# Attention products: which engine takes which heads, a bf16 copy of the softmax weights, and weight conversion in half-size rounds

## The reference

```
xn = layernorm(x)
q, k, v = xn @ wq.T, xn @ wk.T, xn @ wv.T        # each row: 16 heads x 128
q, k = rope(q), rope(k)
scores[s,h,t] = q[s,h,:] . k[s,t,:] / sqrt(128)  # 16 x 16 per row, between the heads of ONE row
attn[s,h,:]   = sum_t softmax_t(scores)[s,h,t] * v[s,t,:]
x = x + attn @ wo.T
y = layernorm(x)
g, u = y @ ((gate_w - 128) * gate_scale).T, y @ ((up_w - 128) * up_scale).T   # int32 weights, 8192 wide
x = x + (silu(g) * u) @ ((down_w - 128) * down_scale).T
```

## Time and profile before

| | us |
|---|---|
| median of 3 runs | 8804.4 |
| lowest and highest run | 8561.8 and 8891.8 |
| the profiled execution | 8532.4 |
| its span on the slowest core (the 8 cores: 8478.5 to 8530.8) | 8530.8 |
| phase A, up to about | 250 |
| phase B, three times, up to about | 1640 |
| phase CD, up to phase E's first matmul | 5072.2 |
| phase E | 3458.6 |

### The profile page before, as it was taken

One profiled execution on the slowest core, in us unless ns is written; L12 is line 12 of the kernel. 1 busy time (PEld: TensorE's weight loads), 2 busy tenths in 40 slices (PEclk: granted clock), 3 DMA queues, 4 the chain that ended last, 5 costly groups with the idle time before them and its releaser, 6 DMA issues.

```text
span 8530.8 us, 45886 instructions; the slowest of 8 cores (8478.5 to 8530.8 us)
## 1 busy us (share of the span) xinstructions
PE 4010.2 (47%) x17408; PEld 1773.4 (21%) x17408; DVE 1869.9 (22%) x1216; ACT 1162.6 (14%) x1257; POOL 1710.7 (20%) x443
## 2 busy tenths in 40 slices
PE   1264636400110111111110139966996699669966
PEld 0121212200000000000000014422442244224422
DVE  2000000044444444444445630000000000000000
ACT  3221212201111111111111011100110011001100
POOL 0000000054444444444446620000000000000000
PEclk9986868755555555555555569977997799779987
DMA  5444454411111111111111026645664566456644
GB/s 179 119 158 128 155 140 145 158 29 62 61 63 65 63 65 61 65 65 68 68 67 69 21 63 152 140 89 134 153 144 89 129 152 147 89 125 154 155 85 108
DMA packets 1714552, 892.33 MB, mean 105 GB/s; under 512 B 1626192, under 2 KB 1634416, under 8 KB 1679520
## 3 DMA queue, kind: packets, MB, share of 16 engines
q1 hardware_dynamic: 1639616, 713.09, 32.8%
q10 hardware_dynamic: 62976, 125.84, 3.8%
q0 software_dynamic: 11744, 50.46, 2.9%
HBM read 755.10 MB, written 167.77 MB: 108 GB/s over the span
## 4 chain that ended last, share of the span: by engine, by line
PE 41%; DMA 20%; POOL 13%; DVE 11%; issue 9%; ACT 5%; ACTq 1%; SPq 0%; DVEq 0%; POOLq 0%
POOL prod L88 13%; PE ps_dn L97 12%; PE ps_g L97 10%; PE ps_u L97 10%; PE ps_p L97 5%; DMA wdb<-wd_sc 5%; DVE prod L88 4%; DVE sc_sb L88 2%; DVE red L88 2%; DMA cvin<-uwT 2%; PE ps_y L97 2%; ACT cvout L88 2%; DMA cvin<-gwT 2%; DMA kt<-k_sc 2%; DMA wg_sc<-cvout 1%
## 5 line engine op out<-in xcount | busy, mean ns | idle before, releaser
L97 PE MATMUL ps_y<-wo_bf,aTs 128*128 128x512 bf16 x1024 | 293.2, 457 | 2587.5 <-ACT yrow_t L88 2281.2
L97 PE MATMUL ps_dn<-h_sb,wdb 128*128 128x512 bf16 x4096 | 1059.1, 427 | 479.9 <-DMA wdb<-wd_sc 474.1
L97 PE MATMUL ps_p<-wst,xnT 128*128 128x512 bf16 x3072 | 769.4, 417 | 622.5 <-ACT prow L88 328.7
L88 DVE TENSOR_REDUCE sc_sb<-prod 128x16 f32<-128x2048 bf16 x256 | 584.2, 2285 | 2073.8 <-POOL prod L88 2065.6
L88 POOL TENSOR_TENSOR prod<-p_sb,vt 128x2048 bf16<-128x2048 f32 x176 | 943.8, 5415 | 356.3 <-DVE p_sb L88 356.3
L97 PE MATMUL ps_g<-xn2q,wgb 128*128 128x512 bf16 x4096 | 934.0, 381 | 66.0 <-DMA wgb<-wg_sc 66.0
L88 POOL TENSOR_TENSOR prod<-qt,kt 128x2048 bf16<-128x2048 bf16 x176 | 720.4, 4132 | 1191.3 <-DMA kt<-k_sc 1154.6
L97 PE MATMUL ps_u<-xn2q,wub 128*128 128x512 bf16 x4096 | 925.8, 379 | 0.8 <-DMA wub<-wu_sc 0.8
L116 POOL DMA_DIRECT2D out_rows<-outt x16 | 8.6, 536 | 3548.9 <-DVE outt L88 3452.6
L88 DVE TENSOR_REDUCE red<-prod 128x128 f32<-128x2048 bf16 x256 | 585.2, 2286 | 591.2 <-POOL prod L88 583.0
L97 PEld LDWEIGHTS ps_y<-wo_bf,aTs 128*128 128x128 bf16 x1024 | 114.2, 114 | 2762.6 <-issue 2687.5
(11 more groups left out here) (52 smaller groups left out, 937.2 us busy)
## 6 DMA issues: line engine op xcount, KB each, us to landing
wgb<-wg_sc SPq DMA_DIRECT2D x256, 512.0 KB, 5.2
wub<-wu_sc SPq DMA_DIRECT2D x256, 512.0 KB, 5.1
wdb<-wd_sc SPq DMA_DIRECT2D x128, 1024.0 KB, 7.0
cvin<-gwT SPq DMA_DIRECT2D x64, 1024.0 KB, 8.0
cvin<-uwT SPq DMA_DIRECT2D x64, 1024.0 KB, 8.3
cvin<-dwT SPq DMA_DIRECT2D x64, 1024.0 KB, 7.6
wg_sc<-cvout ACTq DMA_DIRECT2D x64, 512.0 KB, 2.6
wu_sc<-cvout ACTq DMA_DIRECT2D x64, 512.0 KB, 2.6
```

Of the source, the lines that this page charges most:

```text
L88: ins = getattr(self.h, opname)(*args, **kw)
L97: ins = self.h.matmul(*args, **kw)
```

## The change

Three things are changed, together.

1. **Which engine takes which heads.** VectorE multiplies heads 0 to 4 and GpSimd heads 5 to 15, in both halves of `stage1`. The counts (5 and 11) stay.
2. **A bf16 copy of the weights.** The normalization writes a new tile `pbf` in bf16 in place of overwriting `p_sb`, and the attention products read `pbf`. Its waits for the previous tile's products move from the exponential to the normalization.
3. **Conversion rounds.** A round is 128 x 1024 instead of 128 x 2048: 384 rounds of a 512 KB load and a 256 KB store, with four buffers; a load waits for the conversion four rounds back. There are still two load streams (`b % 2`) and one store stream, so a load also waits for the landing of the load two rounds back. The calls per place go from 2 to 4 (phase A), from 2 to 3 (phase B), and from 3 to 6 (both places of phase CD). That is 32 + 144 + 192 = 368 rounds; the last 16 are left to the drain.

```diff
+        cvin = [cv_sb.enter_context(nc.sbuf_tensor(f"cvin{i}", [128, 1024], I32))
+                for i in range(4)]
...
-                b = r % 2
-                ld = em.dma("sync", f"d_fc{b}", cvin[b][:],
+                b = r % 4
+                ld = em.dma("sync", f"d_fc{b % 2}", cvin[b][:],
...
                 cv = em.do("scalar", "activation", cvout[b][:], cvin[b][:],
                            AF.Copy, bias=-128.0,
-                           waits=[(f"d_fc{b}", ld), ("d_fcs", M["cv_st"][b])])
+                           waits=[(f"d_fc{b % 2}", ld),
+                                  ("d_fcs", M["cv_st"][b])])
...
         def phaseA():
             for g in range(8):
-                conv_step(2)
+                conv_step(4)
...
             for st in range(NT):
-                conv_step(2)
+                conv_step(3)
...
-                    peng = "gpsimd" if hh < POOL_SC else "vector"
+                    peng = "vector" if hh < H - POOL_SC else "gpsimd"
...
                 ex = em.do("scalar", "activation", p_sb[:], sc_sb[:], AF.Exp,
                            scale=INV_SQRT_HD,
-                           waits=[("vector", last_sc), ("vector", M["p_used"]),
-                                  ("gpsimd", M["p_used_g"])])
+                           waits=[("vector", last_sc),
+                                  ("vector", M["p_used"])])
...
-                pn = em.do("vector", "scalar_tensor_tensor", p3, p3, 1.0,
+                pb3 = pbf.ap().rearrange("p (hh t) -> p hh t", hh=H)
+                pn = em.do("vector", "scalar_tensor_tensor", pb3, p3, 1.0,
                            bc_ap(rden_sb, 0, [[1, 16], [0, 16]]),
-                           ALU.mult, ALU.mult, waits=[("vector", rd)])
+                           ALU.mult, ALU.mult,
+                           waits=[("vector", rd), ("gpsimd", M["p_used_g"]),
+                                  ("vector", M["pbf_used_v"])])
...
-                    peng = "gpsimd" if hh < POOL_AT else "vector"
-                    pbc = bc_ap(p_sb, hh * 16, [[0, 128], [1, 16]])
+                    peng = "vector" if hh < H - POOL_AT else "gpsimd"
+                    pbc = bc_ap(pbf, hh * 16, [[0, 128], [1, 16]])
...
-                conv_step(3)
+                conv_step(6)
...
-                conv_step(3)
+                conv_step(6)
```

More of the change, by code:

```diff
@@ L248, in build @@
         cv_sb = contextlib.ExitStack()
[L249 to L252, removed]
+        cvin = [cv_sb.enter_context(nc.sbuf_tensor(f"cvin{i}", [128, 1024], I32))
+                for i in range(4)]
+        cvout = [cv_sb.enter_context(nc.sbuf_tensor(f"cvout{i}", [128, 1024], BF16))
+                 for i in range(4)]
         CONV_ROUNDS = []
@@ L256, in build @@
             for _rh in range(_mat.shape[0] // 128):
-                for _cb in range(_mat.shape[1] // 2048):
+                for _cb in range(_mat.shape[1] // 1024):
                     CONV_ROUNDS.append((_mat, _cache, _rh, _cb))
@@ L267, in conv_step @@
                 mat_ap, cache, rh, cb = CONV_ROUNDS[r]
-                b = r % 2
-                ld = em.dma("sync", f"d_fc{b}", cvin[b][:],
+                b = r % 4
+                ld = em.dma("sync", f"d_fc{b % 2}", cvin[b][:],
                             mat_ap[rh * 128:(rh + 1) * 128,
-                                   cb * 2048:(cb + 1) * 2048],
+                                   cb * 1024:(cb + 1) * 1024],
                             waits=[("scalar", M["cv_m"][b])])
@@ L278, in conv_step @@
                             cache.ap()[rh:rh + 1, :,
-                                       cb * 2048:(cb + 1) * 2048].rearrange(
+                                       cb * 1024:(cb + 1) * 1024].rearrange(
                                 "o p c -> p (o c)"),
@@ L283, in conv_step @@
                 M["conv_done"] = st
-        M.update(cv_r=0, cv_m=[0, 0], cv_st=[0, 0], conv_done=0)
+        M.update(cv_r=0, cv_m=[0] * 4, cv_st=[0] * 4, conv_done=0)
         xnT_scope = contextlib.ExitStack()
@@ L405, in build @@
         p_sb = sbc("p_sb", [128, 256], F32)
+        pbf = sbc("pbf", [128, 256], BF16)
         den_sb = sbc("den_sb", [128, 16], F32)
@@ L427, in build @@
                  sc_done=0, att_done=[0, 0],
-                 exp_done=0, p_used=0, p_used_g=0,
+                 exp_done=0, p_used=0, p_used_g=0, pbf_used_v=0,
                  scp_done_p=[0, 0], scp_done_vv=[0, 0],
@@ L544, in stage1 @@
                 att_last = red_last
-                M["p_used"] = max(pn, atv)
+                M["p_used"] = pn
                 M["p_used_g"] = atg
+                M["pbf_used_v"] = atv
                 M["vt_used"][bi] = atg
```

## The result

| | before | after |
|---|---|---|
| median of all runs (32 of each, side by side) | 8872.9 | 8923.6 |
| lowest run | 8529.0 | 8564.4 |
| ratio of like executions, 95% interval | | 1.0043 [1.0022, 1.0063] |
| the profiled execution | 8532.4 | 8579.0 |
| its span on the slowest core | 8530.8 | 8577.4 |

The change costs 0.4%, about 37 us; a gain of 78 was forecast. In more than half of the executions of either kernel the cores of one die have a lower granted clock and take some per cent longer, which puts the medians above the interval given and above both profiled executions; the ratio compares like with like.

What follows compares the result with a forecast made beforehand. Phase CD bounds it as a chain passing between engines, none near full. Terms of -112.2 (tile 0 to 15), -24.9 (tile 0), +77.1 (tail) and -18 (phase B) sum to -78, from 8532.4 to 8454 us; range 8290 to 8740.

Steps and rivals of the forecast that it cites:

- rival 3: Order of heads, phase CD: if GpSimd wins each contest, the halves end at 59.3 and 86.1, total 8523; 1 in 10.
- bf16: Attention products in phase CD's second half: prices stay at 5.36 and 3.62 us, set by the read step; nothing taken.
- rival 1: Second half of phase CD: bf16 copy cuts products to the scores half's prices, 430 us less, 8024; 2 in 10.
- c: Conversion rounds: time from one store's issue to the next, taken as 2.5 us between bounds 2.06 and 3.43.
- 197 cycles: Store cycles on the path: 16 in phase A, 96 in B, 85 in CD and after it.
- 23 first stores: First store of each conversion group, taken at 4.0 us, half of 8.04, with bounds 2.06 and 8.04.
- idle bound: Lower bound of c, 2.06 us: phase B's 2.71 less 0.65 for 256 KB less, with no competition.
- Rival 2: Conversion rounds: every small store waits behind fresh loads, c = 4.0 everywhere, 296 us more, 8750; 1.5 in 10.
- Phase A: Four small rounds take 10.6 us, about what two large ones took: no change.
- Phase B: Evictions begin 11.25 us after the loads' issue instead of 11.6: -0.37 a tile, -18 us over 48 tiles.
- Phase CD's total: Tile 0's cast to tile 15's: periods of 201.0 us, 2973.2 instead of 3085.4, -112.2 us.
- The tail: After tile 15: groups of 15.6, 14.1 and 14.1, a drain of 43.7, less 10.4: +77.1 us.

## Why the prediction was wrong

- **What bounds the kernel, right.** Phase CD is a chain. Moving the heads alone shortened its halves to 56.8 and 83.7 us, where 57.1 and 84.0 were forecast, and in the kernel after tile 0 came 25.6 earlier for 24.9. The rule read off one collision, that each product holds the other off and they alternate, held in every half of the 16 tiles in which the engines met (only tile 0's scores had no contest); rival 3, the other order, would have given 59.3 and 86.1. One detail was off: VectorE's third product is free (1.22 us), and only its fourth and fifth are stretched.
- **bf16, right in kind.** 5.36 became 5.24 on GpSimd and 3.62 became 3.59 on VectorE. The step stayed and so did the price; rival 1 is out. Taking nothing was 19 us (mean of the cores) to 38 us (slowest cores) off, to the good side. The Trainium skill's Vector Engine (DVE) Microarchitecture Reference, section on measured stream behaviour, puts this cost on the hop; the estimate of 3.5 us worked out from it agrees with the 3.59.
- **The conversion rounds, the step that failed.** The term is c, the time from a store's issue to the next. I took 2.5, "nearer to the idle case, since only one 512 KB load is fresh at each store". Over just those 197 cycles it measured 3.24 on the slowest core: 2.9 in phase B, 3.9 in phase A, 3.3 behind the casts, 3.4 in the three groups behind tile 15, 4.1 in the drain, and single ones from 2.1 to 7.1. That is 146 us. The 23 first stores of a group, taken at 4.0, were 5.5 in phase A and 5.0 behind the casts, another 27. Together these are 173 us, and the rounds alone cost 158 (slowest cores) to 169 us (means) more than their terms. In phase B one fresh load makes the difference between 3.1 and 2.07, as the four load streams showed. In the drain two or more loads were on their way with 11 of the 16 stores, and the cycle was 4.1; that these make it longer still is likely and was not tested. The idle bound was exact and the choice between the bounds wrong. Rival 2, c = 4.0 everywhere, went too far the other way.
- **Phase A, costed at nothing, cost 24 to 31 us.** The prediction had a group's four rounds at 10.6 us; they take 14.7, and the row load of 2 MB is issued at 100.42, beside the last of them. Timeline of one group after, the first conversion and what follows the fourth store:

```profile
89.68 1.04 ACT L88 ACTIVATE cvout<-cvin 128x1024 bf16<-128x1024 int32 x1
...
104.37 1.91 ACT L88 ACTIVATE xbf<-xrow 128x2048 bf16<-128x2048 f32 x1 [4.51 <-DMA wg_sc<-cvout]
```

- **Phase B, wrong sign.** The head of the chain shrank about as forecast: the first conversion came 5.3 us after the loads' issue in place of 6.8, by the mean of all tiles and cores (forecast 4.7 for 6.4). The stores took more than that back: two cycles of 3.7 and 2.4 stand where one of 3.1 stood, and I had 2 x 2.5 for 2.71.
- **Phase CD's total, right by errors that cancel.** The period of 201.3 against 201.0 looks like a hit. By the means of the cores (tiles 1 to 13), the parts alone gave -15.3 (heads), -1.9 (bf16) and +6.2 (rounds), where I had -14.2, 0 and +2.3; their sum is -11.0, together they gave -10.4, and -11.9 was forecast.
- **The tail, mechanism right, size off.** +118.9 for +77.1, 15 x 1.6 = 24 of it in the drain's cycles and most of the rest in the three groups ahead of it, whose cycles were 3.5, 4.1 and 2.9.
- **What hid the risk.** A gain of 238 was set against a cost of 160, and 197 cycles hung on c. The prediction gave the sum for c = 2.06 and for 3.43 (8367 and 8637; the profiled 8579 lies between them), but not the point where the sign turns: 2.5 + 78 / 197 = 2.9, hardly above the value taken and inside the bounds. The chance of no gain should have followed from that, and the forecast should have been nearer to none.
- **The range.** 8290 to 8740 holds the profiled execution and the lowest run, and not the median over all runs, 8923.6: before's own median was 8872.9 in the same runs. I had let the range reach up for the 8804 shown, and not far enough.
- The Trainium skill, DMA: Bandwidth & Descriptors, section on the anatomy of one DMA, gives 2.0 us plus the bytes at 436 GB/s, from which I had estimated c at 2.7; the page fitted this to transfers issued from GpSimd, and these stores are ScalarE's. A 256 KB store without a fresh load had 2.07, below that figure, and one beside fresh loads mostly 3.1 to 5.5, well above it. The same page's rule, to batch to 1 MiB or more, spoke against the edit, and its direction was right.

## What to carry to other kernels

Count how many times a serial wait lies on the path before halving a transfer: the fixed part and the competition are then paid twice as often. Work out the price of one store at which the sign turns, and hold it against the pessimistic bound. A stream in which each transfer waits for the landing of the last can be had in two: that one edit was worth 167 us up to phase E here, over four times the 37.7 that the change lost up to there. And where a stage's hit rests on several terms, run the terms alone before believing it.

## What the runs showed of the hardware

- A VectorE product and a GpSimd product that would run at the same time take turns, one each: a contested VectorE product took 2.69 in place of 1.22 us and 6.29 in place of 3.60, and GpSimd's took 5.0 in place of 4.05 and 8.6 in place of 5.3. VectorE's reductions don't take part: their mean is 2.28 us in the kernel after and 2.29 before.
- The landing of a 256 KB store depends strongly on the loads beside it: a cycle of 2.07 us with no fresh load, 3.1 beside one fresh 512 KB load, and in the drain, with two or more loads on their way beside 11 of the 16 stores, anything from 2.3 to 7.1, 4.1 in the mean. A 512 KB store of the kernel before, with no fresh load, had 2.71.
- With two stores in flight each lands later (medians of the three weights 2.9, 5.3 and 5.8 us in place of 2.3, 3.0 and 3.4), yet the drain's cycle fell from 4.13 to 3.1 us: at 4.13 us the queues had room.
